# Attention loop of a small vision tower: probabilities' copy moved to ScalarE, and a new order of TensorE's work within a step

## What is computed

```python
q, k, v = ...                                   # 8 heads of 8 numbers, 51 tokens
qgr, kgr = qr(q), qr(k)                         # orthonormal factors
dots = einsum('bhnd,bhmd->bhnm', q, k)
a = concat([dots*scale, dots**2*riem_scale, einsum(qgr,kgr)**2*grassman_scale])  # 24 maps
a = conv1x1(batchnorm(a))                       # 24 maps mixed into 8
a = softmax(a, axis=-1)
out = einsum('bhnm,bhmd->bhnd', a, v)
h = h + (out @ w_proj.T + b_proj)
h = h + experts(layernorm(h))                   # router, top 2 of 6 experts
```

## Time and profile before

| | us |
|---|---|
| median of 3 runs | 371.51 (371.2 to 373.81) |
| the profiled execution's own time | 371.06 |
| its span in the profile | 369.3 |
| PE busy | 305.9 (83%) |
| DVE busy | 261.9 (71%) |
| ACT busy | 178.0 (48%) |
| POOL busy | 71.9 (19%) |
| mean granted TensorE clock | 0.902 of full |

### The profile page before, as it was taken

How to read it: one execution, slowest core, us unless ns; L and a number is a source line. 1 busy time by engine, 2 the same in 40 slices (tenths; PEclk the granted TensorE clock), 3 DMA queues, 4 the chain that set the end, 5 groups by cost and what they waited for, 6 DMA issues and landing times.

```text
span 369.3 us, 10042 instructions
## 1 busy us (share of the span) xinstructions
PE 305.9 (83%) x4198; PEld 212.1 (57%) x4198; DVE 261.9 (71%) x595; ACT 178.0 (48%) x309; POOL 71.9 (19%) x67
## 2 busy tenths in 40 slices
PE   4498977788759777878789999989866998999994
PEld 2287564576537655656668776665655544345431
DVE  0887699878787899899964777896988225747241
ACT  0456577622624353534433554848343337595711
POOL 7756424000003222141121231221200000000000
PEclk9799989899867989689988999999998559999989
DMA  8999600000000000000000000000000000010002
GB/s 208 336 328 326 147 0 1 4 4 0 2 0 5 4 2 2 2 3 3 2 4 2 4 2 4 2 3 2 4 2 0 2 0 0 0 26 4 19 0 45
DMA packets 16700, 13.86 MB, mean 38 GB/s; under 512 B 4112, under 2 KB 16400, under 8 KB 16528
## 3 DMA queue, kind: packets, MB, share of 16 engines
q1 hardware_dynamic: 10128, 7.87, 7.8%
q10 hardware_dynamic: 6528, 5.36, 5.2%
HBM read 12.39 MB, written 0.84 MB: 36 GB/s over the span
## 4 chain that ended last, share of the span: by engine, by line
PE 41%; DVE 33%; issue 10%; ACT 9%; ACTq 3%; DMA 1%; POOL 1%; DVEq 0%
PE banks L1373 5%; PE banks L1259 4%; DVE rstd L602 4%; ACT pixels L338 4%; PE banks L1243 4%; ACTq L216 3%; DVE pixels L806 3%; DVE pixels L815 3%; PE banks L1040 2%; DVE pixels L225 2%; PE banks L1270 2%; PE banks L1365 2%; PE banks L1399 2%; PE banks L1284 2%; PE banks L1389 2%
## 5 line engine op out<-in xcount | busy, mean ns | idle before, releaser
L293 POOL TENSOR_TENSOR qbd<-q,weights 128x448 f32<-128x448 f32 x32 | 31.7, 993 | 118.4 <-PE banks L1243 118.3
L1259 PE MATMUL banks<-pixels,convw 64*64 64x204 f32 x768 | 45.1, 367 | 7.3 <-DVE pixels L819 7.3
L1040 PE MATMUL banks<-pixels,weights 128*64 128x204 f32 x416 | 40.8, 359 | 8.6 <-ACT pixels L338 6.4
L1040 PEld LDWEIGHTS banks<-pixels,weights 128*64 128x64 f32 x416 | 35.7, 146 | 14.7 <-issue 11.2
L444 ACT ACTIVATE probs<-pixels 128x408 f32<-128x408 f32 x32 | 17.3, 541 | 52.4 <-DVE pixels L819 52.3
L225 DVE COPY pixels<-pixels 64x1368 f32<-64x1368 f32 x16 | 33.7, 2107 | 12.5 <-DMA pixels<-in_x_dram 12.1
L1259 PEld LDWEIGHTS banks<-pixels,convw 64*64 64x64 f32 x768 | 29.6, 143 | 15.3 <-issue 9.4
L931 DVE TENSOR_TENSOR pixels<-pixels,banks 128x408 f32<-128x408 f32 x24 | 13.6, 576 | 32.9 <-PE banks L1389 20.0
L1243 PE MATMUL banks<-kbd,qbd 64*64 64x102 f32 x1024 | 32.4, 266 | 2.2 <-issue 1.1
L1284 PE MATMUL banks<-vbd,pixels 115*51 115x18 f32 x512 | 18.8, 207 | 15.5 <-DVE pixels L806 13.3
L1284 PEld LDWEIGHTS banks<-vbd,pixels 115*51 115x51 f32 x512 | 15.6, 133 | 26.2 <-DVE pixels L806 21.6
(11 more groups left out here) (161 smaller groups left out, 536.6 us busy)
## 6 DMA issues: line engine op xcount, KB each, us to landing
pixels<-in_x_dram ACTq DMA_DIRECT2D x24, 218.0 KB, 9.9
pixels<-in_x_dram SPq DMA_DIRECT2D x24, 218.0 KB, 11.1
weights<-in_w_dram SPq DMA_DIRECT2D x1, 1200.0 KB, 14.3
out_dram<-pixels SPq DMA_DIRECT2D x8, 102.0 KB
weights<-in_w_dram SPq DMA_DIRECT2D x1, 432.0 KB, 4.0
```

The lines of the kernel that those rows point to most:

```text
L293: pool.tensor_tensor(qbd[u][:, :].rearrange("p (c h i) -> p c h i", c=QB, h=H), qv.unsqueeze(2).to_broadcast([128, QB, H, NI]), w("headmas ...
L1040: last = nc.tensor.matmul(bank[g % 2][64 * half:64 * half + 64, (e % 2) * SN:(e % 2 + 1) * SN], w("tok")[:, v * C:(v + 1) * C], src, start ...
L1259: last = nc.tensor.matmul(bank[2 + r][64 * to:64 * to + 64, 0:4 * N], convw[64 * r:64 * r + 64, k * HI:(k + 1) * HI], src[64 * r:64 * r + ...
```

## The change

Two edits, both inside the loop. First, keys_out leaves VectorE and becomes the first item of ScalarE's step, as an activation with Copy; its waits and its semaphore are the same. Second, TensorE's step has a new order: dots(s), mixing(s-1), values(s-3), transposes(s-2), out-transposes(s-4). So transposes are now made one step earlier in the count, right behind values of the pair before, and keys_out of a pair comes in the step after its transposes.

```diff
@@ scalar
+            def keys_out(s, u, wait):
+                act.wait_ge(S["tr_s"], s + 1)
+                if wait:
+                    act.wait_ge(S["av_s"], s - 1)
+                nc.scalar.activation(pts[u][0:64 + N, :].rearrange("p (h x i) -> p x h i", h=H, i=NI)[:, 0:QB],
+                                     bank[4][0:64 + N, 0:QB * HI].rearrange("p (x h i) -> p x h i", x=QB, h=H),
+                                     ACT.Copy).then_inc(S["pt_s"], 1)
...
             def step(s, u, steady=False):
+                if steady or 3 <= s < PAIRS + 3:
+                    keys_out(s - 3, 1 - u, steady or s >= 5)
                 if steady or 2 <= s < PAIRS + 2:
                     exponentials(s - 2, u, steady or s >= 4)
@@ vector
-            def keys_out(s, u, wait):
-                dve.wait_ge(S["tr_s"], s + 1)
-                if wait:
-                    dve.wait_ge(S["av_s"], s - 1)
-                nc.vector.tensor_copy(...)
...
             def step(s, u, steady=False, between=None):
-                if steady or 3 <= s < PAIRS + 3:
-                    keys_out(s - 3, 1 - u, steady or s >= 5)
                 if between is not None:
                     between()
@@ tensor
                 if steady or s < PAIRS:
                     all_dots(s, u, steady or s >= 1)
-                if steady or 3 <= s < PAIRS + 3:
-                    transposes(s - 3, 1 - u, steady or s >= 4)
                 if steady or 1 <= s < PAIRS + 1:
                     mixing(s - 1, 1 - u, steady or s >= 2)
                 if steady or 3 <= s < PAIRS + 3:
                     values(s - 3, 1 - u, steady or s >= 4)
+                if steady or 2 <= s < PAIRS + 2:
+                    transposes(s - 2, u, steady or s >= 3)
                 if steady or s >= 4:
                     out_transposes(s - 4, u, steady or s >= 5)
```

More of the change, by code:

```diff
@@ L800, in _ @@
             cvec = mixc[:, 15:16]
-            def keys_out(s, u, wait):
-                dve.wait_ge(S["tr_s"], s + 1)
-                if wait:
-                    dve.wait_ge(S["av_s"], s - 1)
-                nc.vector.tensor_copy(pts[u][0:64 + N, :].rearrange("p (h x i) -> p x h i", h=H, i=NI)[:, 0:QB],
-                                      bank[4][0:64 + N, 0:QB * HI].rearrange("p (x h i) -> p x h i", x=QB, h=H))\
-                    .then_inc(S["pt_s"], 1)
             def row_max(s, u, wait):
```

## The result

The changed kernel took 357.49 us in the median of 4 runs (355.77 to 363.22), against 371.36 for the kernel before in 4 runs of the same series: a ratio of 0.960 with an interval of 0.952 to 0.968. Executions of one kernel differ by several microseconds with the clock that they were granted (the changed kernel in a later series: 352.61 us at 0.927, 364.04 at 0.888), so ratios are taken over the faster executions of each kernel, and the medians over all. Forecast were 359.0, in a range of 353.5 to 366. The profiled execution took 355.77 us, its span is 354.0 against 369.3, and its mean granted clock 0.918 against 0.902. The total is near the forecast (13.9 us less, where 12.5 were forecast from 371.51); the parts are not, and most of what follows is about them.

A forecast was written before the change was run, and what follows sets the result against it. PE was taken to bound steps 15 to 20, VectorE mostly steps 3 to 10, with 24 to 34 mixed. Savings of 4.7, 4.7 and 3.3 make 12.7 us off 371.06: 358.4, stated as 359, range 353.5 to 366.

The forecast's parts named there:

- Part 1: Steady steps 15 to 20, bound by PE: no gain, and no new wait.
- their sum stays 3.53: Steady steps: PE's five groups are only reordered, so a step still takes 3.53 us.
- the cover: Steady steps: time between heads_out's end and the start of values, 0.7 us left where there was 1.7.
- Part 2: Steps 3 to 10, up to the row maximum of step 11: VectorE almost without a gap, 4.7 us less.
- 9 x 0.55 = 4.95 us leave its queue: Up to the row maximum of step 11: nine copies of 0.55 us each leave VectorE's queue.
- PE can follow: Steps 3 to 10: PE's 3.53 us per step is below the 4 to 6 us that VectorE still needs.
- first rival: Low clock after longer single PE waits, two more such stretches and a slower expert stage: 366 us, chance 0.12.
- Part 3: Row maximum of step 11 to dots of step 15: 14.3 us instead of 19.0, 4.7 less.
- This is where the order counts: Steps 11 to 14: in the new order nothing of step 13 waits for VectorE's late work; 4.7 us less.
- Part 4: Steps 20 to 34: nine copies off VectorE's path, minus ScalarE lateness 1.1 and low clock 0.5: 3.3 us less.
- the clock gets better: Rival: shorter waits in steps 30 to 34 spare a third of the half-clock stretch behind step 34: 354 us, chance 0.11.
- a mean granted clock below 0.90: Whole kernel: one of the signs named beforehand that would show the prediction wrong.

The follow-up runs named there:

- early ScalarE work: Changed kernel with ScalarE's copy, exponentials and heads_out of steps 23 and 29 moved ahead of square roots and router exponentials: 362.42 us.
- late VectorE work: Changed kernel with VectorE's layer norm and router work of steps 23 to 32 put behind the normalisation, at the step's end: 363.78 us, ratio 0.967.
- heads_out first: Changed kernel with heads_out ahead of the exponentials in steps 23, 27, 28, 29 and 33: 355.68 us, ratio 0.955.
- extra copy: Changed kernel plus one 115x448 copy into an unread spare buffer, first on VectorE in steps 3 to 34: 367.91 us, ratio 0.987.

## Why the prediction was right, and where it was not

Five traces (the changed kernel twice, and those with early ScalarE work, late VectorE work and heads_out first) are of the same program up to step 22. Three are of kernels with the copy on VectorE (the kernel before twice and the new order alone). That gives the spread of each part:

| part | copy on VectorE | copy on ScalarE | gain | forecast |
|---|---|---|---|---|
| 2: dots 0 to row maximum 11 | 58.96, 57.09, 58.61 | 55.74, 57.53, 55.00, 58.46, 58.31 | 58.2 - 57.0 = 1.2 | 4.7 |
| 3: to dots 15 | 19.02, 19.01, 20.12 | 15.08, 13.72, 14.04, 13.73, 15.06 | 19.4 - 14.3 = 5.1 | 4.7 |

**Part 1 failed at "their sum stays 3.53".** No wait came in, the copy took 0.540 us (0.54 was taken) and the cover held, even for a second copy that held ScalarE 0.44 us longer. But the sum itself depends on the order: 3.18 us. Five steps (15 to 20) gain 1.77 us by it. In the steps behind them nothing of it is left: dots 20 to 24 take 19.13 us before and 19.02 after, though the new order alone has 18.15. The copy on ScalarE gives it back there, since values wait for heads_out in steps 22 and 23 (0.49 and 1.36 us).

**Part 2 failed at the term "9 x 0.55 = 4.95 us leave its queue" and at "PE can follow".** The profiled pair shows 3.2 and the mean over eight executions 1.2, with 3.5 between the fastest and slowest of equal programs; so the gain lies below 4.7, and by how much stays uncertain. (Two more kernels with the copy on ScalarE and other orders on TensorE took 55.39 and 56.31 us.) Where the rest went can be seen between the row maxima of steps 3 and 11, where eight copies had held VectorE for 8 x 0.55 = 4.4 us. First, its busy time fell by less: by 3.15 in the pair (38.17 to 35.02 us) and by 1.9 in the mean of the eight (37.6 to 35.7), because it ran into POOL more often. In the changed kernel, for instance, the second of two equal operations on 128x4 numbers stands beside POOL's block queries:

```profile
169.08 0.17 DVE L697 TENSOR_TENSOR pixels<-pixels 128x4 f32<-128x4 f32 x1
169.28 0.87 DVE L700 TENSOR_TENSOR pixels<-pixels 128x4 f32<-128x4 f32 x1
169.08 1.04 POOL L293 TENSOR_TENSOR qbd<-q,weights 128x448 f32<-128x448 f32 x1 [8.50 <-PE banks L1243]
```

I counted the VectorE instructions in this stretch that took over 0.1 us more than the shortest of their shape. All of them overlap an instruction of POOL. With the copy on VectorE there are 5 or 6, for 2.4 to 3.8 us in sum; with it on ScalarE 8 to 10, for 4.9 to 6.8. So the contention that I had put at no net change, with 1.5 either way, took about 2.4 of the 4.4 us. Second, VectorE idled more. The stretch shrank by 0.9 in the mean (42.1 to 41.2), so its idle time grew by 1.0. That idle time was 4.9 and 3.6 us in the two executions with a granted clock of 0.87 and 0.89, and 6.5, 5.6 and 6.4 in those with 0.77, 0.77 and 0.82; these took 41.9, 42.5 and 42.4 us, against 39.9 and 39.1. With the copy on VectorE the clock was 0.88, 0.92 and 0.86. This fits the first rival ("low clock takes part of it back") inside part 2, though no run isolates it: the wait in one piece, 3.41 us ahead of the mixing of step 8, and low clock behind it. The extra copy on VectorE shows the same from the other side: in this stretch its 4.4 us cost 1.0.

Low clock in the second execution of the changed kernel, from 160 to 170 us:

```profile
160.00:170.00 10.00, 7.69 (x102) 6.22 (x102) 8.65 (x34) 4.52 (x9) 1.04 (x1) 0.51 0.01 2
```

In the first execution it is 0.66 there. Whether the new order brings such stretches more often, or three and five executions happened to differ, stays open.

**Part 3 was right in size, partly by luck, and wrong in cause.** The 14.3 us from the row maximum of step 11 are the mean of five executions to the tenth, but no execution took that: three at full clock took 13.7 to 14.0, two at 0.89 took 15.1. At full clock the chain from mixing to the dots of step 14 is 8.4 us and not 9.1, and the step behind it 3.18 and not 3.53, because the new order shortens the groups and the key products take 2.0 and not 2.25; against that the mixing begins 0.45 to 0.8 late, behind a small addition (L819 in the changed kernel) that took 0.67 to 1.00 us in place of 0.23. And "This is where the order counts" is refuted: with the new order alone the part takes 20.1 us, and with the copy alone 14.6. What counted was that keys_out no longer stands behind `block_m(1)`, and not VectorE's load, as the extra copy shows (14.6).

**Part 4 was too low.** The profiled pair gives 4.5 instead of 3.3, and the mean of two executions of each kernel 5.3 (68.58 and 71.70 against 64.05 and 65.67). Its own sum has a slip, since 0.78 and 0.43 make 1.2 and not 1.1. VectorE's copies at about 0.5 each are borne out by the extra copy. The two places where ScalarE would be late are there (0.49 in step 22, forecast as 0.78), with more that I had not seen, above all 1.36 in step 23; that step's price was set at the dots of step 24 and it came at values. In the two steps that were tried, 23 and 29, the waits are in the main not ScalarE's own: moved away, most of them come back ahead of mixing, behind the layer norm's and router's work on both engines.

**Behind step 34** nothing was changed, and the times of all profiled executions are 79.7 to 81.6 us, or 85.0 to 86.1. The kernel before has both, 81.64 and 84.95, and so has the changed one, 79.80 and 86.05. The granted clock from 305 to 354 us is 1.00 in the one and 0.87 in the other execution of the changed kernel:

```profile
305.00:354.00 49.00, 46.93 (x159) 20.40 (x158) 20.51 (x56) 26.06 (x47) 0.00 (x0) 0.87 0.05 10
```

So the 1.8 us of the first table are nobody's gain, and the rival "the clock gets better" is not what happened: the stretch that it spoke of stayed at low clock.

```profile
272.90:289.30 16.40, 15.53 (x43) 8.41 (x43) 3.67 (x8) 4.68 (x10) 0.00 (x0) 0.51 0.01 1
```

In sum: 12.7 us were forecast for the loop. 13.5 came in the first pair, 13.1 in the mean of two executions of each kernel (164.23 and 165.47 against 150.77 and 152.82). The 359 was right by luck, because errors met: in the first pair part 2 was put too high by 1.5 and part 3 by 0.8, part 1 too low by 1.8 and part 4 by 1.2; by the means part 2 was too high by 3.5, parts 1, 3 and 4 too low by 1.8, 0.4 and 2.0. One sign of being wrong, a mean granted clock below 0.90, came in four of the ten executions of the changed kernel (0.873 and three times 0.888), and these too were faster than any execution of the kernel before. It was no good sign, since the kernel before itself has 0.890 in its second trace.

The rule of the Trainium skill that spoke against the edit ("ScalarE: Activation LUTs", Rules for kernel authors) gives its factor of three for bf16 and did not hold for this fp32 read out of PSUM: ScalarE's 0.540 us is less than VectorE's 0.62 in rows 3. The figure of 186 ns plus 0.833 ns per element there (What ACT_TABLE_LOAD costs), 0.56 us by an estimate, is 4% above the measured time. The copy's group line in the changed kernel's profile:

```profile
L451 ACT ACTIVATE pixels<-banks 115x448 f32<-115x448 f32 x32 | 17.3, 540 | 16.0 <-PE banks L1270 16.0
```

## What to carry to other kernels

Moving an operation to a less busy engine pays only if its producers stand early enough: here the copy's new home delayed every steady step until the transposes were moved as well, and neither edit alone was worth what both were. Look at what stands ahead of an operation in its engine's queue, more than at the engine's busy share: the 4 to 5 us of part 3 came from one copy that stood behind a 2.85 us piece of other work. Where an engine is busy nearly all the time, time taken out of its queue is still an upper bound of the gain and not the gain: here 4.4 us taken out gave 0.9 in the mean and 2.8 in the first pair. And a wait that one sees for an engine may be the far end of a chain through others; before moving work to remove it, follow that chain.

## What was not expected of the hardware

The time of a group of matmuls depended on the group beside it. With dots next to mixing (both 64*64) and transposes next to out-transposes (128*115 and 115*128) the same instructions took 3.18 us instead of 3.53, at full clock and with nothing waited for; with only the first of these pairs together, 3.38. Ordering the groups of this PE-bound step so was worth 10% of it.

Equal programs took up to 3.5 us more or less up to step 11, and 6 us behind step 34, where the granted clock was 1.00 in one execution and 0.87 in the other. A single pair of profiles would have made 3.2 us of a part that is worth about 1.2 in the mean.
